# Output projection's head products in groups of 4, 7 and 3 with two left behind gate and up, and VectorE's last gate block ahead of the third block's product

## The reference

```python
x = x + xattn(layernorm(x), ctx, Wq, Wk, Wv, Wo, gq, gk)   # 16 heads of 128, softmax, out @ Wo
x = x + ffn(layernorm(x), w_gate, w_up, w_down)

def h_bitlinear(x, w):
    xq = act_quant(fwht(x))          # Hadamard rotation, 8-bit absmax per token
    wq = weight_quant(w)             # ternary weights
    return einsum('bsh,oh->bso', xq, wq)

gate, up = h_bitlinear(x, w_gate), h_bitlinear(x, w_up)
return h_bitlinear(silu(gate) * up, w_down)
```

## Time and profile before

| | us |
|---|---|
| median of 3 runs | 1381.54 |
| lowest and highest run | 1379.87 and 1381.78 |
| the profiled execution's own time | 1381.65 |
| its span in the profile | 1379.8 |

### The profile page before, as it was taken

One profiled execution on the slowest core, in us unless ns is written; L12 is line 12 of the kernel. 1 busy time (PEld: TensorE's weight loads), 2 busy tenths in 40 slices (PEclk: granted clock), 3 DMA queues, 4 the chain that ended last, 5 costly groups with the idle time before them and its releaser, 6 DMA issues. The chain is left out here.

```text
span 1379.8 us, 28300 instructions
## 1 busy us (share of the span) xinstructions
PE 1359.2 (99%) x9496; PEld 1212.2 (88%) x9496; DVE 917.1 (66%) x2414; ACT 918.1 (67%) x2019; POOL 540.6 (39%) x477
## 2 busy tenths in 40 slices
PE   9999989999999999999999999999999999999997
PEld 9899867999999999999999999998978887888885
DVE  6312046667777777777777777766558778887886
ACT  5556568878888888888888888787734433444342
POOL 1034326433233323323332423324735555555551
PEclk9999999999999999999999999999999999999999
DMA  8867813333444444444434443434462342334212
GB/s 250 234 186 202 231 55 111 110 105 110 135 114 129 120 120 120 140 114 117 138 113 122 129 120 118 121 102 137 153 189 55 90 88 62 70 76 102 62 32 43
DMA packets 186403, 166.36 MB, mean 121 GB/s; under 512 B 87938, under 2 KB 155540, under 8 KB 184468
## 3 DMA queue, kind: packets, MB, share of 16 engines
q1 hardware_dynamic: 178980, 151.50, 39.9%
q10 hardware_dynamic: 7280, 13.06, 3.6%
HBM read 124.57 MB, written 33.02 MB: 114 GB/s over the span
## 5 line engine op out<-in xcount | busy, mean ns | idle before, releaser
L804 POOL TENSOR_TENSOR rk_sp<-ms_sp,neg_half 124x6 f32<-124x6 f32 x128 | 169.8, 1354 | 465.9 <-DMA ms_sp<-ms 465.9
L1237 DVE CUSTOM_DVE_ANT_0 sc<-psS,rk 100x361 f32<-100x361 f32 x256 | 136.6, 533 | 131.4 <-PE psS L889 92.8
L1032 ACT ACTIVATE pr<-ex,ri 100x361 f32<-100x361 f32 x256 | 152.5, 596 | 42.8 <-DVE ri L1225 42.8
L1025 ACT ACTIVATE ex<-sc,nb,rq_all 100x361 f32<-100x361 f32 x256 | 174.8, 683 | 2.9 <-DVE nb L1246 2.9
L917 PE MATMUL psZ<-pT_hi,cK_hi 120*128 120x400 f32 (+1 forms) x384 | 132.7, 346 | 0.0
L917 PE MATMUL psZ<-pT_hi,cK_lo 120*128 120x400 f32 (+1 forms) x384 | 132.1, 344 | 0.0
L917 PE MATMUL psZ<-pT_lo,cK_hi 120*128 120x400 f32 (+1 forms) x384 | 131.9, 344 | 0.0
L1007 ACT ACTIVATE ring_hi<-bank 128x362 fp32r<-128x362 f32 x128 | 60.5, 473 | 77.8 <-PE bank L865 77.0
L902 PEld LDWEIGHTS psP<-ident,pr 100*120 100x120 f32 (+1 forms) x768 | 73.5, 138 | 43.5 <-issue 35.3
L1217 DVE TENSOR_TENSOR pT_lo<-psP,pT_hi 122x600 fp32r<-122x600 f32 x128 | 98.9, 773 | 1.2 <-ACT pT_hi L1056 1.1
L932 PE MATMUL psNV<-z,wv_sb 128*128 128x200 f32 x504 | 97.2, 336 | 0.8 <-issue 0.8
(11 more groups left out here) (315 smaller groups left out, 3895.9 us busy)
## 6 DMA issues: line engine op xcount, KB each, us to landing
rk<-rk_dram SPq DMA_DIRECT2D x128, 290.6 KB
q_dram<-q_out SPq DMA_DIRECT2D x64, 200.0 KB, 4.4
q_in<-q_dram SPq DMA_DIRECT2D x64, 200.0 KB, 3.9
o_dram<-o SPq DMA_DIRECT2D x64, 200.0 KB, 4.3
stage<-in_w_ff SPq DMA_DIRECT2D x12, 1024.0 KB, 6.4
w_in<-in_w_ff ACTq DMA_DIRECT2D x48, 256.0 KB, 3.9
o_in<-o_dram SPq DMA_DIRECT2D x12, 1024.0 KB, 5.9
cT_in<-in_ctxT SPq DMA_DIRECT2D x15, 361.0 KB, 4.0
```

What stands on the lines that cost most here:

```text
L804: nc.gpsimd.tensor_tensor(rk_sp[:, cols], ms_sp[:, cols], neg_half[0:HG * SKR, :].to_broadcast([HG * SKR, n]), op=ALU.pow).then_inc(g_rk, 1)
L1025: nc.scalar.activation(ex[:, h % 2, :], sc[:, h % 2, :], ACT.Exp, bias=nb[:, h % 2:h % 2 + 1], scale=factor(n), accum_out=rs[:, h % 2:h % ...
L1032: nc.scalar.activation(pr[:, h, SKP - SK:SKP], ex[:, h % 2, :], ACT.Copy, scale=ri[:, h % 2:h % 2 + 1]).then_inc(a_pr, 1)
L1237: nc.vector.tensor_tensor_reduce(out=sc[:, h % 2, :], in0=psS[0:SQ, 0:SK], in1=rk[:, u % 2, h, 0:SK], scale=1.0, scalar=-3.0e38, op0=ALU.m ...
```

## The change

Two edits, both in `feed_forward`:

- `AHEAD` goes from 12 to 14. The groups of `out_high(i + 3)` become heads 0 to 3, 4 to 10 and 11 to 13 in place of 0 to 2, 3 to 8 and 9 to 11, and two heads in place of four are left behind gate and up.
- On VectorE the order `gate(2), hidden(2), gate(3), hidden(3)` becomes `gate(2), gate(3), hidden(2), hidden(3)`. Nothing else moves, and no operation is added or removed.

```diff
-        AHEAD, FIRST = 12, 8
+        AHEAD, FIRST = 14, 8
...
                 if real(i + 3):
-                    out_high(i + 3, range(0, 3))
+                    out_high(i + 3, range(0, 4))
                 elif i == TILES - 3:
                     busy(psA, 5)
                 if real(i + 2):
                     rotate_in(i + 2)
                 if real(i + 3):
-                    out_high(i + 3, range(3, 9))
+                    out_high(i + 3, range(4, 11))
                 elif i == TILES - 3:
                     busy(psA, 11)
                 if real(i + 2):
                     q1_T(i + 2)
                 if real(i + 3):
-                    out_high(i + 3, range(9, AHEAD))
+                    out_high(i + 3, range(11, AHEAD))
...
                 if real(i + 1):
-                    for n in range(NB):
+                    for n in range(NB - 1):
                         gate(i + 1, n)
                         if n == 0 and real(i):
                             ints2(i, 1)
-                        hidden(i + 1, n)
+                        if n < NB - 2:
+                            hidden(i + 1, n)
+                    gate(i + 1, NB - 1)
+                    hidden(i + 1, NB - 2)
+                    hidden(i + 1, NB - 1)
                     rotate_within(i + 1, 2)
                     rotate_within(i + 1, 3)
```

## The result

| | before | changed |
|---|---|---|
| median of 14 runs, us | 1381.66 | 1384.79 |
| lowest and highest, us | 1379.87 and 1384.54 | 1383.51 and 1386.71 |
| span of the profiled execution, us | 1379.8 | 1383.0 |

The ratio is 1.0023 with a 95% interval of 1.0016 to 1.0030: 3.1 us slower, where 2.7 were forecast. It is inside the range, and just beyond the 0.2% (2.8 us) that the prediction took as the bound of what can be told. In microseconds the interval is 2.2 to 4.1.

A forecast was written before the change was run, and what follows sets the result against it. TensorE leads throughout, busy 27.79 of 27.91 us in a step. Ten full steps add 2.3 us, step -1 adds 0.46, step 10 takes off 0.05: + 2.7, forecast 1384.2 us, range 1381.2 to 1386.1.

The forecast's parts named there:

- Both waits: TensorE waits 0.29 us ahead of rotate_in's second product and 0.27 ahead of q1_T; both go, 0.56 us of a step.
- Step -1: The step ahead of the ten full steps, where rotation block 2 already waits: 0.46 us longer in all.
- step 10: The step after the ten full ones, with no heads behind norm_T, which waits there for xr: 0.05 us shorter.
- the sum: Ten full steps at 0.23 us more make 2.3; with step -1 and step 10, + 2.7 us.
- The reserve of block 2: TensorE's rotation block 2 has 0.07 to 0.08 us before it must wait for the third hT_lo; TensorE reaches it 0.92 earlier.
- VectorE's order: hidden(3) ends 0.77 us earlier, but GpSimd's rotate_pair0 holds rotate_within(2) until 9.27, so 0.05 is left.
- The faster rival: VectorE's rotations are not held up, its chain is 0.77 us earlier: total - 5.9, 1375.6 us, chance 0.13.
- The partly held case: VectorE's rotations are slowed at a rate of 70% of the overlap, 0.17 us won: 1382.8 us, chance 0.13.
- The late release: VectorE's rotate_within(2) starts only at GpSimd's shown end, 9.40; 1.6 us more, 1385.8 us, chance 0.17.

The follow-up runs named there:

- the heads alone: The changed kernel without its edit in VectorE's step, so VectorE in the old order: 1385.14 us against 1381.38, ratio 1.0025.
- the cut: The changed kernel with GpSimd's second operation of rotate_pair0 cut from 512 columns to 8: 1376.98 us against 1381.38, ratio 0.9967.
- its control: The changed kernel with VectorE's old order and GpSimd's second rotate_pair0 operation at 8 columns: 1384.82 us against 1381.05, ratio 1.0028.
- the memset: The changed kernel with GpSimd's second rotate_pair0 operation replaced by a memset that only writes SBUF: 1377.14 us against 1382.23, ratio 0.9961.
- the half operation: The changed kernel with GpSimd's second operation of rotate_pair0 at 256 of 512 columns: 1378.45 us against 1382.23, ratio 0.9975.

## Why the prediction was right

- **The waits and the moved heads.** Both waits went, and the groups overfilled them. `rotate_in` stands 0.17 later, as forecast. `q1_T` stands 0.20 later in the step shown and 0.23 on the mean of the ten, where 0.19 was forecast: this is the term that was too small. The distances between the head products ahead of `q1_T` are 0.229 us on the mean in three of the steps and 0.231 in seven, against 0.227 to 0.229 before; what spreads them is not known. With `norm_T` at 0.11 earlier instead of 0.12, a step came out at 0.29 longer and not 0.23, and the ten at 2.94 and not 2.3.
- **The total.** Step -1 is 0.49 longer, where 0.46 was forecast, and step 10 is 0.03 shorter, where it was 0.05. So by the two profiles these twelve steps take 3.4 us more, where the sum has 2.7. The medians differ by 3.1, with an interval of 2.2 to 4.1, which holds both. That the medians came out nearer to the sum than these steps did is luck.
- **The reserve of block 2.** It was 0.07 us against 0.92 moved, and the heads alone show what that means: 0.32 us lost in each step with no other edit. `norm_T` comes only 0.08 us earlier there, so nearly all of the 0.92 turns into waiting.
- **VectorE's order.** `hidden(3)` came 0.73 us earlier, where 0.77 was forecast, and of this 0.05 was left behind the rotations, as forecast. The reason, GpSimd's second operation, is shown by the cut and its control; that it holds until 0.13 us ahead of its shown end, and not at a rate, by the two sizes; that it is its reading, by the memset.
- **The rivals.** The faster rival has 5.9 us less than before, 1375.6; with the operation cut, the run has 4.4 less than before on its chip, 1377.0, with an interval of 2.9 to 6.4. In the ten steps it is 3.95 us where the rival has 4.9. So the rival was wrong in its condition, and its price a little too high. Its steps would be 27.42 us and are 27.52: block 2 is released at 17.26 and not at 17.22, `norm_T` follows it 0.02 later, and `q1_T` pays its 0.04. The partly held case falls with the half operation. The late release falls with the shown 0.13.
- **The border.** The forecast lay just inside the 0.2%, 2.7 against 2.8 us, and the result, 3.1, just outside. The result's interval, 2.2 to 4.1, holds both, so which side of the bound it fell on says nothing about the mechanism.
- **A reading.** The prediction puts GpSimd's power beside the `xn` at 1148.90. The power had ended at 1148.79, so that 0.54 is the length of an `xn` with nothing beside it. The argument is not changed.

## What to carry to other kernels

Before an operation is brought forward, look at what the other of VectorE and GpSimd does at its new time, and not only at its old one. Here a GpSimd operation of 512 columns that reads SBUF held a VectorE operation with two SBUF inputs until 0.13 us ahead of its shown end, and this shows as a longer operation and not as a wait. Before work is moved away from ahead of a point, read the reserve at that point; filling a wait of 0.3 with a piece of 0.46 from a place that has no reserve is a loss, and the same piece from a place that has reserve (the third group) was worth 4 us here, a third of it from the collision that it undid. Where an expected order gives more than its own wait, look for a second collision that it undid.

## What the runs showed of the hardware

GpSimd's hold ends about 0.13 us ahead of its shown end, in three sizes (2.31, 1.30 and 0.75 us). VectorE's `q`, an operation with one SBUF input that turns fp32 into bf16 at 512 columns in 0.42 us, is longer beside GpSimd's `y` too: 0.57 when it comes 0.28 ahead of its end, 0.47 when 0.19 ahead, 0.42 when 0.11 ahead, which fits the same 0.13. So was `xn` in the earlier trace rows, but its 1.51 less the usual 0.54 puts its start in effect 0.26 ahead of the end of `y`, so 0.13 is not the same for every pair. Two inputs from SBUF are therefore not the only case. The gate and hidden products, with one input from PSUM and one from SBUF, were never held: none takes over 0.70 us.

Nor does every GpSimd operation that reads SBUF hold VectorE. The power of the layer norm, one column wide, in the kernel before:

```profile
1147.86 0.93 POOL L1463 TENSOR_TENSOR rstd<-ve,neg_half 128x1 f32<-128x1 f32 x1 [2.95 <-DVE ve L1852]
```

As its span is shown, it runs beside the last two `hT_lo` of the step (1147.70, 1.28 for both in the earlier trace rows), and the second of them begins in the middle of it. In all twelve steps these take 0.68 to 0.69 us each, their usual time, though both their inputs are in SBUF.
